# A one-core megakernel of retention, attention and channel mix: retention scores on 64-row halves, first row maxima on four banks, VectorE work reordered

## The chip, the cores and the metric

One core of one Trainium2 chip. The time is the device time of one execution in microseconds (us), and the metric is the median over runs. The engines are TensorE (PE in the profile, PEld for its weight loads), VectorE (DVE), ScalarE (ACT), GpSimd (POOL) and SyncE (SP), which issues most DMAs.

## The reference

Eight sequences of 1024 tokens with 256 channels, all in float32. What matters of it:

```
x = x + retention(layernorm(x))      # 4 heads, dk 64, dv 128
x = x + ffn(layernorm(x))            # channel mix: r * (relu(k)^2 @ W_v)
x = x + attention(layernorm(x))      # 16 heads of 16, relative bias, softmax
x = x + ffn(layernorm(x))

# retention, chunk by chunk (the kernel uses chunks of 128)
attn = (q @ k^T) * Dmask
o = attn @ v + (q * cross) @ S
S = S * gC + (k * kdec)^T @ v
o = rmsnorm(o) * silu(g);  out = x + o @ Wo
```

The attention's softmax subtracts the true maximum of each row of scores (query), so scores are computed twice: once by rows, to get the maxima, and once by columns (keys on partitions) with the maximum folded in as an extra row of the operands.

## The kernel before

Each sequence goes through five stages, and each engine's program is written out by hand, with semaphores (`need`, `reach`, `wait_ge`) between them. An engine runs its instructions in order, so the order written in the code is the order of the work. A product of plain float32 operands is two passes of PE, one with `F32R` operands is one.

**Retention** (loop `for t in range(1, NT + 1)` on PE; NT = 8 tiles of 128 tokens). DVE makes the normalised tile (`z_norms`, L1466), PE transposes it (`z_transposes`, L637), ACT copies it with the layer norm's weights (`z_copies`, L1310), and DVE takes the low part (`z_lows`, L1617). `project` (L643, L647) makes q and k (bank 0), v (bank 1) and the gate g (bank 2), six products of 512 columns each. DVE rotates q and k (`rope`, L1639 and L1645), POOL adds and scales (L1909, L1916), PE transposes them into bank 3 (`qk_transposes`, L1027), and ACT copies them out in three operations (L1358 to L1360): q of two heads goes to `qbd`, whose other halves are zeros, so that one product on all 128 rows serves two heads (block diagonal), and k goes to `kT`. For tile u = t - 1 PE then makes the scores (L1058, two products of 256 columns into bank 4), DVE masks them into `AT` (L1668), and PE makes the outputs in bank 5: per head `AT` times v (L1082) and, for u > 0, `qbd` times the state S (L1085). L1092 is the update of the state, on column halves (64 output rows each) of the array; DVE adds it to S (L1690, L1693). ACT squares the outputs (L1348), POOL makes the reciprocal root (L1924, L1928), ACT takes tanh of g (L1353), DVE makes the gate (L1703) and the gated outputs y (L1710). y is transposed (`y_transposes`, L977), copied and split (L1332, `y_lows` L1623), projected (`y_project`, L991, twelve products of 256 columns) and added to x (`x_out`, L1630), three tiles later.

**First channel mix** (`mix_k` L683, `mix_r` L707, `mix_kv` L725, with layer norms `ln_stats`, `ln_norms` L1590, `ln_transposes` L666, `ln_copies` L1257; POOL squares in L1863 and adds in L1872). **Attention's projections** (`qk_project` L831, `v_project` L843). SP spreads q and k to `SQ` and `SK` through DMAs, 64 rows of partitions for each head: even heads on partitions 0 to 63, odd ones on 64 to 127.

**Ahead stage** (`last_mix_and_rows`): the first AHEAD = 22 of 128 units of row products, put between the second channel mix of the sequence before. A unit is one head and one tile of queries, and has two products of 512 columns, k = 0 and 1 (`score_rows`, L868). DVE takes the maximum of each (`row_max`, L1755). Row products take banks 0 to 2 in turn. After 16 units the maxima of a block are folded (L1759), transposed (`max_transpose`, L882), copied (L1401) and written into `SQ` by DMA (`max_rows_in`, L450). In the DVE program statistics, norms, mixes and gated products of the sequence before are hung between the units by number.

**Attention** (64 steps): two more units of rows per step until all are done, four column products (`score_cols`, L899), exponentials on ACT (L1430), the bias band on POOL (L1964), and the weighting with v (`weigh`, L924), on column quarters. At its end the next sequence's first projections begin, with its `rope(b + 1, 0)`.

In the set-up of the first sequence DVE makes constants (L1516 to L1521) and the bias tables (`bias_tables`, L1548 to L1558) ahead of its loop.

## Time and profile before

| | us |
|---|---|
| median of 3 runs | 2854.99 (2853.36 to 2856.19) |
| the profiled execution, its own time | 2854.48 |
| its span in the profile | 2852.6 |
| PE busy | 2752.4 |
| DVE busy | 2115.9 |
| ACT busy | 1775.8 |
| POOL busy | 1266.7 |

Busy time of PE counts from a matmul's start to its modelled end; as matmuls are pipelined, the next one starts before that, and a row of the timeline with several of them (x8) shows the start of the first and the time to the end of the last. So the distance between the starts of two rows is what the first of them took. [...] The rows below are mostly from one inner sequence, the one whose retention stage begins at 1066.6 us.

### The profile page before, as it was taken

The numbers are of one execution on the slowest core, as the hardware profiler recorded it, in microseconds if no ns is written. First come the engines' busy times: TensorE is split into PE (matmuls) and PEld (weight loads), VectorE is DVE, ScalarE is ACT, GpSimd is POOL, SyncE is SP. The second block draws the span as 40 slices with busy tenths as digits, with TensorE's granted clock in tenths as the row PEclk, the third lists the DMA queues.
The fourth block names the chain that finished last, engine by engine and source line by source line (L and its number), as shares of the span: only waits on it lengthen the run. The fifth ranks groups of instructions, "written<-read, shape, count | busy, mean of one in ns | idle before, by whom it ended". The sixth has DMA issues, their size and how long they took to land.

```text
span 2852.6 us, 53205 instructions
## 1 busy us (share of the span) xinstructions
PE 2752.4 (96%) x19426; PEld 1526.9 (54%) x19426; DVE 2115.9 (74%) x4444; ACT 1775.8 (62%) x3799; POOL 1266.7 (44%) x1764
## 2 busy tenths in 40 slices
PE   7989999999999999999999999999999999999998
PEld 5733376433864348643486434854358533585334
DVE  6679756897568965689666995669956799567993
ACT  5438854488545875458754687536875378653785
POOL 3415544355433554335543445434454345433553
PEclk9979999999999999999999999999999999999999
DMA  7160001600025000250002400033000330003300
GB/s 191 31 133 2 24 9 41 137 17 24 9 50 128 17 31 1 60 119 17 31 1 74 105 17 31 1 90 88 17 31 10 101 69 17 31 30 89 60 2 16
DMA packets 71428, 139.16 MB, mean 49 GB/s; under 512 B 12784, under 2 KB 49696, under 8 KB 70016
## 3 DMA queue, kind: packets, MB, share of 16 engines
q1 hardware_dynamic: 69152, 135.29, 19.1%
q8 instruction: 156, 2.56, 0.4%
q14 instruction: 104, 0.85, 0.1%
q10 hardware_dynamic: 2016, 0.45, 0.1%
HBM read 86.02 MB, written 38.82 MB: 44 GB/s over the span
## 4 chain that ended last, share of the span: by engine, by line
PE 71%; DVE 14%; issue 6%; POOL 5%; SPq 1%; ACT 1%; DMA 1%; POOLq 0%; DVEq 0%; ACTq 0%
PE psum L868 20%; PE psum L924 16%; DVE mx L1755 6%; PE psum L643 5%; PE psum L991 3%; PE psum L899 3%; PE psum L831 3%; PE psum L647 2%; PE psum L707 2%; PE psum L683 2%; PE psum L1085 2%; PE psum L1082 2%; DVE nrm L1590 2%; PE psum L1058 1%; POOL X L1872 1%
## 5 line engine op out<-in xcount | busy, mean ns | idle before, releaser
L1755 DVE TENSOR_REDUCE mx<-psum 128x1 f32<-128x512 f32 x2048 | 1266.2, 685 | 87.4 <-PE psum L868 87.0
L1430 ACT ACTIVATE Z<-psum 128x512 f32<-128x512 f32 x2048 | 1109.6, 598 | 279.7 <-PE psum L899 252.6
L1964 POOL TENSOR_TENSOR Z<-Z,W_low 128x256 f32<-128x256 f32 (+1 forms) x1152 | 713.0, 642 | 687.2 <-ACT Z L1430 679.9
L868 PE MATMUL psum<-SK,SQ 63*128 63x512 f32 x2048 | 801.2, 471 | 28.5 <-DVE mx L1755 23.0
L899 PE MATMUL psum<-SQ,SK 64*128 64x512 f32 x2048 | 758.6, 472 | 8.1 <-DMA SQ<-mrow 7.5
L924 PE MATMUL psum<-Z,Vx 128*17 128x256 f32 x8192 | 642.0, 388 | 0.4 <-POOL Z L1964 0.4
L868 PEld LDWEIGHTS psum<-SK,SQ 63*128 63x128 f32 x2048 | 330.0, 191 | 480.8 <-DVE mx L1755 357.9
L899 PEld LDWEIGHTS psum<-SQ,SK 64*128 64x128 f32 x2048 | 311.4, 189 | 79.9 <-ACT Z L1430 37.5
L924 PEld LDWEIGHTS psum<-Z,Vx 128*17 128x17 f32 x8192 | 138.3, 95 | 334.8 <-issue 274.8
L1909 POOL TENSOR_TENSOR Z<-Z 128x512 f32<-128x512 f32 x64 | 83.6, 1306 | 295.6 <-DVE Z L1645 295.6
L1872 POOL TENSOR_TENSOR X<-X,mixed 128x512 f32<-128x512 f32 x64 | 80.4, 1268 | 235.3 <-DVE mixed L1611 235.3
L643 PE MATMUL psum<-W_high,zT_both 128*128 128x512 f32 x384 | 170.2, 443 | 0.5 <-ACT Z L1310 0.5
L643 PE MATMUL psum<-W_low,zT_both 128*128 128x512 f32 x384 | 152.2, 396 | 0.0
L1348 ACT ACTIVATE Z<-psum 128x128 f32<-128x128 f32 x256 | 67.2, 277 | 125.0 <-PE psum L1085 122.6
L683 PE MATMUL psum<-xkT,WT 128*128 128x512 f32 x256 | 126.3, 613 | 4.0 <-DVE xkT L1601 2.1
L707 PE MATMUL psum<-WT,xrT 128*128 128x256 f32 x512 | 126.5, 389 | 0.0
L831 PE MATMUL psum<-nT,WT 128*128 128x512 f32 x256 | 115.8, 600 | 6.6 <-ACT nT L1257 6.6
L647 PE MATMUL psum<-W_high,zT_both 128*128 128x512 f32 x384 | 120.1, 394 | 0.0
L1283 ACT ACTIVATE mixed<-psum 128x512 f32<-128x512 f32 x64 | 38.2, 597 | 130.0 <-PE psum L707 130.0
L707 PEld LDWEIGHTS psum<-WT,xrT 128*128 128x128 f32 x512 | 92.6, 189 | 32.4 <-issue 22.6
L1590 DVE TENSOR_SCALAR nrm<-X,fmv,frs 128x256 f32<-128x256 f32 x192 | 73.8, 446 | 43.7 <-POOL frs L1858 43.7
L1310 ACT ACTIVATE zT_both<-psum,vec 128x128 fp32r<-128x128 f32 x128 | 51.6, 454 | 83.8 <-PE psum L637 83.3
(138 smaller groups left out, 3716.8 us busy)
## 6 DMA issues: line engine op xcount, KB each, us to landing
W_low<-bias_rows SPq DMA_DIRECT2D x8, 2048.0 KB, 8.6
parts<-Z SPq DMA_DIRECT2D x32, 512.0 KB
W_low<-low_parts SPq DMA_DIRECT2D x7, 1536.0 KB, 6.7
X<-L_attn_a_x SPq DMA_DIRECT2D x8, 1024.0 KB, 5.6
SQ<-parts SPq DMA_DIRECT2D x32, 256.0 KB, 7.9
SK<-parts SPq DMA_DIRECT2D x32, 256.0 KB, 10.7
SQ<-parts SPq DMA_DIRECT2D x16, 512.0 KB, 6.6
SK<-parts SPq DMA_DIRECT2D x16, 512.0 KB, 14.5
```

What stands on the lines that cost most here:

```text
L643: pe.matmul(bank[dst], zT_parts[0][:, t % 2, c, :], Wqkvg_parts[part][:, c, c0:c0 + 512], start=c == 0 and part == 0, stop=False)
L647: mm = pe.matmul(bank[dst], zT_parts[1][:, t % 2, c, :], Wqkvg_parts[0][:, c, c0:c0 + 512], start=False, stop=c == C - 1)
L683: mm = pe.matmul(k_bank(b, q, o), WT[:, W_K, c, o * P:o * P + P], xkT[:, c, :], start=c == 0, stop=c == C - 1)
L707: mm = pe.matmul(bank[4 + pr][:, i * D:i * D + D], xrT[:, c, t * P:t * P + P], WT[:, W_R, c, :], start=c == 0, stop=c == C - 1)
L831: mm = pe.matmul(bank[QK_BANK[n % 2]], WT[:, A_Q + side, c, h * P:h * P + P], nT[:, c, 1 + 512 * g:513 + 512 * g], start=c == 0, stop=c == ...
L868: pe.matmul(row_bank(c), SQ[rows_of(h, MAX_ROW), h // 2, i * P:i * P + P], SK[rows_of(h, MAX_ROW), h // 2, 512 * k:512 * k + 512], start=T ...
L899: pe.matmul(col_bank(n), SK[rows_of(h), h // 2, j * P:j * P + P], SQ[rows_of(h), h // 2, 512 * half:512 * half + 512], start=True, stop=Tr ...
L924: mm = pe.matmul(sum_bank(s // 8)[32 * c:32 * c + HD + 1, cols], Vx[:, j, 4 * hg + c, :], ring[:, (4 * s + cols_of(s).index(c)) % RING, cols],
L1430: nc.scalar.activation(ring[:, n % RING, :], col_bank(n), ACT.Exp)\
L1590: nc.vector.tensor_scalar(nrm[:, i, :], X_of[b % 2][:, 4 * g + i, :], fmv[:, i, 0:1], frs[:, i:i + 1], ALU.subtract, ALU.mult).then_inc(fn ...
L1755: nc.vector.tensor_reduce(mx2[:, blk % 2, col, k:k + 1], row_bank(2 * u + k), AX_X, ALU.max)\
L1964: nc.gpsimd.tensor_tensor(ring[:, n % RING, a:z], ring[:, n % RING, a:z], band_exp[:, 4 * hg + cols_of(s)[i], at:at + z - a], ALU.mult)\
```

## The change

- `qbd` and `kT` give way to one tile `qkT` (q and k of the tile, all 128 rows, no zeros), which ACT fills with one copy. Two heads of a pair lie on its rows 0 to 63 and 64 to 127. The scores are now, in the new function `scores`, four products of 128 columns on 64 rows each, for the even heads into bank 4 and for the odd ones into bank 5. q times S follows in the same function, also on 64 rows, into the columns 256 to 511 of the same banks; `outputs` adds `AT` times v to it. DVE masks both banks in one operation (`by_side`), and ACT and DVE read the outputs with `o_of(h)`.
- PE's order in a tile: the v projection goes ahead of the scores; from tile 3 on the next transposes of z stand between them. At t = 2 the states go ahead of the outputs. `scores` waits for the gated outputs of the tile before.
- DVE's order: `rope(b, t)` ahead of the mask, `rope(b, 1)` out of the loop, behind the last norm of the sequence's start (in the first sequence ahead of `constants` and `bias_tables`); `ln_stats(b, 0)` and `ln_norms(b, 0)` earlier, the gated outputs at t = 7 ahead of the gate; `z_norms(b, 3)` at t = 1.
- Ahead stage: `row_product` orders the first 44 row products so that the same k of two units follows one another, and with that two halves of the rows; banks 0 to 3 in turn for the first 40 of them. The layer norm of the second half of the mix (`ln_transposes(b - 1, 5)`) stands earlier, on banks 6 and 7; mixes and gated products hang at other units; the first block's transpose goes to bank 4.
- In the last mix `mix_kv` waits for the copies of that norm, and ACT makes them ahead of the tanhs.

The diff, cut to its core:

```diff
-qbd = sb("qbd", [P, 2, 2, 2, P])
+qkT = sb("qkT", [P, 2, 4, P])
...
-LN_BANK = (0, 0, 0, 0, 4, 3)
+LN_BANK = (0, 0, 0, 0, 4, 6)
...
+def o_of(h):
+
+    return bank[4 + h % 2][:, 256 + h // 2 * DV:256 + h // 2 * DV + DV]
+
...
+def row_product(c):
+    if c < 2 * AHEAD:
+        return c // 4 * 2 + c % 2, c % 4 // 2
+    return c // 2, c % 2
+ROW_BANKS = [c % 4 if c < 2 * AHEAD - 4 else c % 3 for c in range(2 * NU)]
+LAST_ROW = [max((m for m in range(c) if ROW_BANKS[m] == ROW_BANKS[c]), default=None) for c in range(2 * NU)]
 def row_bank(c):
-    return bank[c % 3]
+    return bank[ROW_BANKS[c]]
...
-            need(pe, c_lo, min(b + 1, B - 1), 8)
+            pe.wait_ge(k_relu, 2 * mix_at(b, 2) + 2)
         for c in range(C):
-            if n == 5 and c == 1:
-                pe.wait_ge(r_tanh, 2 * mix_at(b, 2) + 1)
...
+        if q == 2:
+            pe.wait_ge(fn_T, 2 * norm_at(b, 5) + 2)
...
-            for u in range(rows, rows + n):
-                score_rows(b, u, 0)
-                score_rows(b, u, 1)
+            for c in range(2 * rows, 2 * rows + 2 * n):
+                score_rows(b, c)
...
             mix_r(b - 1, 2, 0, (0,))
             some_rows(1)
+            ln_transposes(b - 1, 5)
             mix_r(b - 1, 2, 0, (1,))
...
-            ln_transposes(b - 1, 5)
...
-        if b > 0:
+            mix_kv(b - 1, 3, 0, (0,))
+            max_transpose(b, 0)
+            some_rows(1)
+            mix_kv(b - 1, 3, 0, (1,))
+            some_rows(1)
             mix_kv(b - 1, 3, 1, (0,))
             some_rows(1)
             mix_kv(b - 1, 3, 1, (1,))
+        else:
+            some_rows(17 - rows)
+            max_transpose(b, 0)
         some_rows(AHEAD - rows)
...
+
+        u, k = row_product(c)
         h, i, _, _ = unit(u)
-        c = 2 * u + k
         if k == 0:
             rows_wait(b, u)
         if c == 0:
             pe.wait_ge(fn_T, 2 * norm_at(b, 3) + 2)
-        elif c > 2:
-            need(pe, mx_r, b, c - 2)
+        if c == 3:
+            need(pe, c_lo, b, 8)
+        if LAST_ROW[c] is not None:
+            need(pe, mx_r, b, LAST_ROW[c] + 1)
...
+        if n == 0:
+            need(pe, mx_r, b, 2 * AHEAD - 4)
...
+    def scores(b, u):
+        need(pe, kq_T, b, u + 1)
+        need(pe, att_m, b, u)
+        need(pe, s_upd, b, 2 * u)
+        need(pe, y_h, b, 4 * u)
+        if u == 0:
+            need(pe, z_T, b, 8)
+            need(pe, w_T, b - 1, 1)
+        for pr in range(2):
+            for side in range(2):
+                r = slice(DK * side, DK * side + DK)
+                mm = pe.matmul(bank[4 + side][:, P * pr:P * pr + P], qkT[r, u % 2, 2 + pr, :],
+                               qkT[r, u % 2, pr, :], start=pr == 0, stop=False, skip_group_check=True)
+        if u > 0:
+            for pr in range(2):
+                for side in range(2):
+                    r = slice(DK * side, DK * side + DK)
+                    mm = pe.matmul(o_of(2 * pr + side), qkT[r, u % 2, pr, :], S[r, pr, :],
+                                   start=False, stop=False, skip_group_check=True)
+        mm.then_inc(att.sem, 1)
+    def outputs(b, u):
+        need(pe, att_m, b, u + 1)
+        need(pe, v_cp, b, u + 1)
+        for h in range(RET_HEADS):
+            mm = pe.matmul(o_of(h), AT[:, h * P:h * P + P], v_sb[:, u % 2, h * DV:h * DV + DV],
+                           start=False, stop=h >= 2, skip_group_check=True)
+        mm.then_inc(p_o.sem, 1)
+    def states(b, u):
+        need(pe, v_cp, b, u + 1)
+        need(pe, s_upd, b, 2 * u)
+        need(pe, z_T, b, 4 * min(u + 3, NT))
+        for h in range(RET_HEADS):
+            mm = pe.matmul(bank[6][64 * (h % 2):64 * (h % 2) + 64, (h // 2) * DV:(h // 2) * DV + DV],
+                           qkr[:, u % 2, 256 + h * DK:256 + h * DK + DK],
+                           v_sb[:, u % 2, h * DV:h * DV + DV], start=True, stop=True,
+                           skip_group_check=True)
+        mm.then_inc(p_st.sem, 1)
...
+            u = t - 1
+            if t == 1:
+                scores(b, u)
+            if t <= 2:
                 z_transposes(b, t + 1)
+            if t < NT:
                 need(pe, v_cp, b, t)
                 if t == 1:
                     need(pe, x_att, b - 1, 3)
                 project(b, t, 1, 512, p_v)
+            if 3 <= t < NT - 1:
+                z_transposes(b, t + 1)
+            if t >= 2:
+                scores(b, u)
+            if t >= 3:
                 y_project(b, t - 3)
             if t == NT:
                 y_transposes(b, NT - 2)
+            if t == 2:
+                states(b, u)
+            outputs(b, u)
+            if t != 2 and t < NT:
+                states(b, u)
             if t < NT:
...
-                quad = bank[3].rearrange("p (a n) -> p a n", a=4)
-                nc.scalar.copy(qbd[0:64, t % 2, :, 0, :], quad[0:64, 0:2, :]).then_inc(kq_T.sem, 1)
-                nc.scalar.copy(qbd[64:128, t % 2, :, 1, :], quad[64:128, 0:2, :]).then_inc(kq_T.sem, 1)
-                nc.scalar.copy(kT[:, t % 2, :, :], quad[:, 2:4, :]).then_inc(kq_T.sem, 1)
+                nc.scalar.copy(qkT[:, t % 2, :, :], bank[3].rearrange("p (a n) -> p a n", a=4)).then_inc(kq_T.sem, 1)
...
+    def by_side(w):
+
+        return w[:, :].rearrange("p (c a n) -> p a c n", a=2, c=2)
...
     z_lows(0, 1)
     z_norms(0, 2)
+    rope(0, 1)
     constants()
     bias_tables()
     for b in range(B):
         for t in range(NT + 1):
-            if 1 < t < NT - 1:
+            if 2 < t < NT - 1:
                 z_norms(b, t + 1)
             if 3 <= t and t != 7:
                 y_lows(b, t - 3)
+            if 2 <= t < NT:
+                rope(b, t)
             if 1 <= t:
                 u = t - 1
                 need(dve, att, b, u + 1)
                 need(dve, p_o, b, u)
-                nc.vector.tensor_tensor(AT[:, :], bank[4], mask[:, :], ALU.mult)\
+                nc.vector.tensor_tensor(by_side(AT), psum[:, 4:6, 0:256].rearrange("p a (c n) -> p a c n", c=2),
+                                        by_side(mask), ALU.mult)\
                     .then_inc(att_m.sem, 1)
-            if 0 < t < NT:
-                rope(b, t)
+            if t == 1:
+                z_norms(b, 3)
             if t >= 3:
                 x_out(b, t - 3)
             if 0 < t < NT - 1:
                 z_lows(b, t + 1)
+            if t == 6:
+                ln_stats(b, 0)
+            if t == 7:
+                ln_norms(b, 0)
...
             if t == 7:
-                ln_norms(b, 0)
+                gated_outputs(b, u)
             if b == 0 and 3 <= t < 7:
                 bias_rows(2 * t - 5)
             if t < NT:
-                need(dve, p_g, b, t + 1)
-                need(dve, g_tanh, b, t + 1)
-                nc.vector.scalar_tensor_tensor(gt[:, t % 2, :], gt[:, t % 2, :], 1.0, bank[2],
-                                               ALU.add, ALU.mult).then_inc(gate.sem, 1)
-            if 1 <= t <= NT:
-                need(dve, o_rs, b, u + 1)
-                need(dve, gate, b, u + 1)
-                need(dve, y_tp, b, u)
-                for h in range(RET_HEADS):
-                    nc.vector.scalar_tensor_tensor(y[:, h * DV:h * DV + DV], bank[5][:, h * DV:h * DV + DV],
-                                                   ors[:, u % 2, h:h + 1], gt[:, u % 2, h * DV:h * DV + DV],
-                                                   ALU.mult, ALU.mult).then_inc(y_h.sem, 1)
+                gates(b, t)
+            if 1 <= t <= NT and t != 7:
+                gated_outputs(b, u)
...
-                    mixes(b - 1, 3, (0,), (0,))
-                elif u == 8:
-                    mixes(b - 1, 3, (0,), (1,))
+                    mixes(b - 1, 3, (0,))
+                elif u == 9:
                     gated(b - 1, 2, (0,))
-                elif u == 9:
+                elif u == 10:
                     gated(b - 1, 2, (1,))
-                elif u == 11:
+                elif u == 12:
                     mixes(b - 1, 3, (1,))
-                elif u == 16:
+                elif u == 18:
                     gated(b - 1, 3, (0,))
-                elif u == 17:
+                elif u == 20:
                     gated(b - 1, 3, (1,))
...
             z_lows(b + 1, 1)
             z_norms(b + 1, 2)
+            rope(b + 1, 1)
...
-                need(pool, att, b, t)
+                need(pool, p_st, b, max(t - 1, 0))
```

## Rows read from the trace of the kernel before

**Rows 1.** The page: span, and busy time of the engines.

```profile
span 2852.6 us, 53205 instructions
...
PE 2752.4 (96%) x19426; PEld 1526.9 (54%) x19426; DVE 2115.9 (74%) x4444; ACT 1775.8 (62%) x3799; POOL 1266.7 (44%) x1764
```

**Rows 2.** The page: the chain that ended last, by line.

```profile
PE psum L868 20%; PE psum L924 16%; DVE mx L1755 6%; PE psum L643 5%; PE psum L991 3%; PE psum L899 3%; PE psum L831 3%; PE psum L647 2%; PE psum L707 2%; PE psum L683 2%; PE psum L1085 2%; PE psum L1082 2%; DVE nrm L1590 2%; PE psum L1058 1%; POOL X L1872 1%
```

**Rows 3.** Busy time by stretch: us, engines' busy us (instructions), clock, DMA.

```profile
1066.60:1149.60 83.00, 81.94 (x535) 70.30 (x532) 49.48 (x129) 42.98 (x138) 33.53 (x40) 1.00 0.02 6
...
1201.60:1244.80 43.20, 41.98 (x142) 22.82 (x142) 36.08 (x67) 9.91 (x17) 10.96 (x10) 1.00 0.55 146
...
1209.80:1246.50 36.70, 35.41 (x124) 19.68 (x123) 29.68 (x50) 8.83 (x16) 9.02 (x8) 0.99 0.58 155
...
1246.50:1387.00 140.50, 138.37 (x1287) 50.97 (x1285) 136.08 (x252) 120.34 (x226) 74.91 (x120) 0.98 0.15 31
```

**Rows 4.** Waits in 1201.6 to 1244.8: who for whom, us, times, longest.

```profile
DVE mx L1755 <- PE psum L868: 5.9, 8, 2.0
```

**Rows 5.** Timeline, PE, tile 0 and 1 of retention: start us, us, instruction.

```profile
1080.13 1.05 PE L1082 MATMUL psum<-Z 128*128 128x128 f32 x8
...
1081.11 0.66 PE L1092 MATMUL psum<-Z 128*64 128x128 f32 x8
...
1082.04 0.39 PE L643 MATMUL psum<-W_low,zT_both 128*128 128x512 f32 x1
...
1084.09 0.66 PE L1027 MATMUL psum<-ident,Z 128*128 128x128 f32 x4 [0.74 <-POOL Z L1916]
```

**Rows 6.** Timeline, PE, a tile of retention with a state.

```profile
1115.08 1.03 PE L1058 MATMUL psum<-qbd,Z 128*128 128x256 f32 x4
...
1115.94 0.38 PE L637 MATMUL psum<-ident,Z 128*128 128x128 f32 x2
...
1118.96 0.38 PE L1082 MATMUL psum<-Z 128*128 128x128 f32 x2
...
1120.84 0.66 PE L1092 MATMUL psum<-Z 128*64 128x128 f32 x8
```

**Rows 7.** Timeline, ACT and DVE, the same stretch.

```profile
1110.84 0.28 ACT L1348 ACTIVATE Z<-psum 128x128 f32<-128x128 f32 x1 [2.60 <-PE psum L1085]
...
1114.32 1.12 DVE L1710 SCALAR_TENSOR_TENSOR Z<-psum,ors,Z 128x128 f32<-128x128 f32 x4
...
1116.28 0.68 DVE L1668 TENSOR_TENSOR Z<-psum,mask 128x512 f32<-128x512 f32 x1
```

**Rows 8.** Timeline, PE and DVE, ahead stage.

```profile
1209.93 1.13 PE L707 MATMUL psum<-WT,xrT 128*128 128x256 f32 x4
...
1210.99 0.73 PE L868 MATMUL psum<-SK,SQ 63*128 63x512 f32 x2
...
1211.65 1.13 PE L707 MATMUL psum<-WT,xrT 128*128 128x256 f32 x4
...
1241.01 5.47 DVE L1755 TENSOR_REDUCE mx<-psum 128x1 f32<-128x512 f32 x9
```

**Rows 9.** Timeline, PE, attention stage, two products on opposite halves.

```profile
702.73 0.49 PE L899 MATMUL psum<-SQ,SK 64*128 64x512 f32 x2
```

**Rows 10.** Timeline, PE and DVE, set-up of the first sequence.

```profile
30.07 0.62 PE L647 MATMUL psum<-W_high,zT_both 128*128 128x512 f32 x2
...
27.80 0.29 DVE L1516 TENSOR_SCALAR nrm<-nrm,vec 128x128 f32<-128x128 f32 x1 [0.54 <-DMA cbias<-L_attn_b_bo]
...
32.26 0.41 DVE L1558 COPY xrT<-xrT 64x64 f32<-64x64 f32 x2
...
35.01 1.05 PE L1082 MATMUL psum<-Z 128*128 128x128 f32 x8
```

**Rows 11.** Busy time by stretch, as in 3: first sequence, and one attention begin.

```profile
157.10:193.70 36.60, 26.77 (x56) 12.56 (x56) 27.46 (x46) 0.96 (x3) 0.00 (x0) 0.59 0.54 150
...
1246.00:1252.90 6.90, 6.90 (x28) 2.96 (x28) 6.10 (x11) 5.31 (x11) 4.20 (x6) 0.51 1.05 156
```

More of the change, by code:

```diff
@@ L424, in max_bank @@
         def max_bank(blk):
-            return sum_bank(blk) if blk else bank[3]
+            return sum_bank(blk) if blk else bank[4]
         def rows_of(h, n=HALF):
@@ L692, in mix_r @@
                 reach(pe, r_tanh, 2 * at + pr - 1)
-                if q == 0 and pr == 0:
-                    need(pe, att_m, b, NT)
-                if q == 0 and pr == 1:
+                if q == 0:
                     need(pe, y_h, b, 4 * NT)
@@ L875, in max_transpose @@
                 if blk == 0:
-                    need(pe, c_lo, b, 8)
-                    pe.wait_ge(fn_T, 2 * (norm_at(b - 1, 5) if b > 0 else norm_at(b, 3)) + 2)
+                    need(pe, vx_cp, b, 4)
+                    if b > 0:
+                        pe.wait_ge(r_tanh, 2 * mix_at(b - 1, 3) + 1)
                 elif blk == 1:
@@ L1106, in _ @@
                 need(pe, gate, b, NT)
-                need(pe, kq_T, b, 3 * NT)
+                need(pe, kq_T, b, NT)
                 mix_k(b, 0, 0)
@@ L1347, in _ @@
                         for h in range(RET_HEADS):
-                            nc.scalar.activation(sq_junk[:, h * DV:h * DV + DV], bank[5][:, h * DV:h * DV + DV], ACT.Square,
+                            nc.scalar.activation(sq_junk[:, h * DV:h * DV + DV], o_of(h), ACT.Square,
                                                  accum_out=oss[:, u % 2, h:h + 1]).then_inc(o_sq.sem, 1)
@@ L1487, in ln1_scales @@
                     .then_inc(ln1_sc.sem, 1)
-            for dst, value in ((power[:, :], -0.5), (nT[:, :, 0:1], 0.0), (qbd[:, :, :, :, :], 0.0),
+            for dst, value in ((power[:, :], -0.5), (nT[:, :, 0:1], 0.0),
                                (Vx[:, :, :, HD:HD + 1], 1.0), (S[:, :, :], 0.0), (nrm[:, 0, :], 1.0)):
@@ L1646, in rope, with gates, gated_outputs @@
                         .then_inc(rope_ab.sem, 1)
+            def gates(b, t):
+                need(dve, p_g, b, t + 1)
+                need(dve, g_tanh, b, t + 1)
+                nc.vector.scalar_tensor_tensor(gt[:, t % 2, :], gt[:, t % 2, :], 1.0, bank[2],
+                                               ALU.add, ALU.mult).then_inc(gate.sem, 1)
+            def gated_outputs(b, u):
+                need(dve, o_rs, b, u + 1)
+                need(dve, gate, b, u + 1)
+                need(dve, y_tp, b, u)
+                for h in range(RET_HEADS):
+                    nc.vector.scalar_tensor_tensor(y[:, h * DV:h * DV + DV], o_of(h),
+                                                   ors[:, u % 2, h:h + 1], gt[:, u % 2, h * DV:h * DV + DV],
+                                                   ALU.mult, ALU.mult).then_inc(y_h.sem, 1)
             z_lows(0, 0)
@@ L1749, in _, with row_max @@
                         mixes(b - 1, 2, (1,))
-                def row_max(u):
-                    _, _, blk, col = unit(u)
-                    for k in range(2):
-                        need(dve, mx_s, b, 2 * u + k + 1)
-                        nc.vector.tensor_reduce(mx2[:, blk % 2, col, k:k + 1], row_bank(2 * u + k), AX_X, ALU.max)\
+                def row_max(n):
+                    for c in (2 * n, 2 * n + 1):
+                        u, k = row_product(c)
+                        _, _, blk, col = unit(u)
+                        need(dve, mx_s, b, c + 1)
+                        nc.vector.tensor_reduce(mx2[:, blk % 2, col, k:k + 1], row_bank(c), AX_X, ALU.max)\
                             .then_inc(mx_r.sem, 1)
-                    if u % 16 == 15:
-                        need(dve, mx_r, b, 2 * u + 2)
+                    if n % 16 == 15:
+                        need(dve, mx_r, b, 2 * n + 2)
                         nc.vector.tensor_reduce(mx[:, blk, :], mx2[:, blk % 2], AX_X, ALU.max).then_inc(mx_f.sem, 1)
```

66 lines of the change are left out of this document (11 added, 55 removed).

## The prediction

> **What bounds the kernel now.** I read the page first, then the chain, the stage table, the waits, and last the timeline. TensorE (PE) is busy 96% of 2852.6 us [rows 1], but its ends are modelled, so the chain decides: it runs through PE matmuls, and the row-maximum line of VectorE (DVE) is its third place [rows 2]. The stages of one inner sequence [rows 3] then differ. In the retention stage (83.0 us) PE is busy 81.94 and its weight loads 70.30; DVE only 49.48. In the ahead stage (43.2 us, 22 units of first row products between the previous sequence's channel mix) DVE has 36.08. In the attention stage DVE has 136.08 of 140.5: the row maxima bound it, and whatever ends the ahead stage's maxima earlier should move all that follows. In the ahead stage DVE waits 5.9 us for row products [rows 4]: PE is the later one there.
>
> **Retention, PE work removed.** A full-array pass of 128 columns follows the next in 0.111 us: eight take 0.98 us to the first of the state update, which includes the step into column halves [rows 5]. Scores before are two products of 256 columns, 0.86 us [rows 6]. The outputs of a tile with a state are 16 passes in 1.88 us, 0.1 of it the same step, so 1.78 [rows 6]; eight of them are q times S on a half-empty array. After, scores and q times S are 16 passes on 64 rows, even heads in bank 4 and odd in bank 5. If two run side by side that is 8 x 0.111 = 0.89 us in place of 0.86 + 0.89 = 1.75. No row shows 64-row passes of this kind, but two neighbours do the same thing: the state update, on column halves, takes its eight passes and the first projection product in 0.93 us where serial ones would need 8 x 0.111 + 0.23 = 1.12 before any overhead [rows 5], and two 512-column products on opposite row halves end within 0.49 us, two on one half within 0.73 [rows 8, 9].
>
> The step into and out of halves costs time. From the same rows: 0.98 - 0.89 = 0.09 going in, and 0.93 - 0.445 - 0.23 = 0.25 inside and coming out: 0.34 per visit. The new `scores` adds one visit per tile. So a tile with a state saves 1.75 - 0.89 - 0.34 = 0.52 us, the first tile 0.86 - 0.445 - 0.34 = 0.07. Per sequence 7 x 0.52 + 0.07 = 3.7 us. Bounds: nothing pairs (below), or the visit costs as little as 0.1 (2 us more per sequence).
>
> [...]
>
> **Retention, waits moved.** Scores of tile u now stand behind the v projection and overwrite what the outputs of u-1 were read from, so they wait for the gated outputs of u-1. That chain is squares on ScalarE (ACT), a power on GpSimd (POOL), four DVE products: 1110.84 to 1115.44, 4.6 us after the outputs end [rows 7]. PE has the states, gate projection, transposes, q/k and v projections, about 6 us, in between: hidden, with some 1.3 us over. The mask (0.68 [rows 7], about 1.0 with the latency of PE's last pass) lies behind the y projection (12 x 0.115 = 1.4 us) from the fourth tile on: hidden. At t = 2 only the state update (0.6) covers it: 0.3 lost. At t = 8 DVE does gated outputs, gate and the low part of y in a row (1.12 + 0.69 + 0.68, forms as in [rows 7]) before PE can go on with the y projection: 0.7 lost. One copy in place of three after the q/k transposes frees ACT, which isn't late anyway: nothing. The second rope moved ahead of the loop takes away the 0.74 us (0.9 with the restart) that PE waits for POOL at t = 1 [rows 5], in seven sequences. Net per inner sequence 3.7 - 0.3 - 0.7 + 0.9 = 3.6; seven make 25 us. No DMA is moved or added.
>
> **The first sequence's set-up.** rope(0, 1) now stands ahead of the constants and bias tables on DVE and waits for a projection that ends at 30.7. The constants and tables took 27.80 to 32.67, in DVE's idle time [rows 10]; now rope takes 1.45 and they follow: 30.75 + 1.45 + 4.9 = 37.1. Gate and mask (0.69 + 0.68) end at 38.6, and the outputs that ran at 35.01 [rows 10] start at 38.7: 3.7 later. The rest of that sequence's gain (3.7 - 1.0 + 0.4) pays most of it; with PE idle some 4 us I add 1.5 for a possible fall of the clock. Net 2 us lost. [...]
>
> **The ahead stage.** Between 1209.93 and 1211.65 PE does four passes (0.86 us) and one unit of rows: the unit costs 0.86 us, of which 0.46 are two products one after the other (k = 0 and 1 of one head, one half) and 0.40 switching [rows 8]. In the new order `some_rows(1)` issues the same k of an even and an odd head, which pair: 0.23 + about 0.30 = 0.53. 22 units save 7.3 us of PE. Added up from 1202.2: before 23.3 us of other matmuls + 22 x 0.86 = 42.2, which is the stage's length; after 35. DVE's own work there, 44 maxima at 0.608 (nine in 5.47 us [rows 8]) = 26.8, statistics 1.8, norms 1.4, mixes 2.8, gated products 2.7, takes 35.5 from 1203.2: it would end at 1238.7 without a wait, and ends at 1246.5 now. So DVE becomes the bound. Going through the new order unit by unit (four banks let PE be two units ahead; transposes of norm 5 on banks 6 and 7, ready right after unit 5; r mixes late by 1.8 us at unit 14, PE waiting), I get the last maximum at 1241.1: 5.4 us earlier. I take 5.0; bounds 2 and 7.7 (all of DVE's idle time, 36.7 - 29.7 [rows 3], and a little at its start). Seven sequences: 35 us. In the first sequence DVE and the copy-in of the row maxima bound the stage: nothing. The attention stage itself is unchanged and moves ahead whole. The last sequence's mix loses 1.5 us: its second half now waits for two ACT copies of norm 5 before the product with W_V (two operations near the 0.7 of [rows 7]).
>
> **Sum.** -25 + 2 - 35 + 1.5 = -56.5 us. The profiled execution took 2854.5 (span 2852.6), 0.5 below the median of the runs, 2855.0. 2854.5 - 56.5 = **2798 us**.
>
> **Rivals.**
> (A) The 64-row passes don't pair. Then each tile with a state gives 0.89 back, the first 0.445: 6.7 a sequence, 53 in all: 2851, within 0.2% of before. For it: no row has 128-column passes with a 128-column load each on row halves, and two loads must fit in 0.11 us. Against: [rows 5, 9]. Chance 0.04.
> (B) The ahead stage gives little, because DVE or the load of the row maxima holds the attention stage's begin (2 us instead of 5 a sequence, less where mixes are late): 21 less, 2819; with further waits in retention, up to 2832. For it: the margin between PE's 35.0 and DVE's 35.5 is nothing, so every late mix shows. Chance 0.15.
> (C) Slower: the clock. [...] Chance 0.05.
> **Numbers.** Main case 0.76 (its own range 2784 to 2814, from the bounds of visit and ahead stage), B 0.15, A 0.04, C 0.05. 0.2% (5.7 us) is what a measurement can tell from no change. Faster 0.92, same 0.03, slower 0.05. The range leaves out the low tail, A and C, and takes in B: 2782 to 2832.
>
> **What would show it.** Right: in a steady tile the new line of the scores has 16 passes in about 1.2 us; the tile's period falls from 10.1 to 9.6; `L1027` has no wait at t = 1; a unit of rows in the ahead stage costs 0.5 us and DVE has hardly any wait there; retention 79.5 and ahead stage 38 us long; DVE ends its first 44 maxima 5 us earlier; PE idle 4 us around 35 to 38. Wrong: passes at 0.111 each in the scores (A); PE waiting for gated outputs or mask in every tile; granted clock below 1 inside the ahead stage (C); ACT or a load ending the wait of the first column product (B).

## The result and the profile after

The changed kernel takes **2825.38 us** (median of 4 runs, 2824.51 to 2830.58) against 2855.26 for the kernel before on the same chip: ratio 0.9901, 95% interval 0.9889 to 0.9913. Of the 57 us forecast, 30 came. The direction was right, the time lies in the range, and the size was wrong: about half.

The page of after, span and engines, then the chain by line:

```profile
span 2822.7 us, 53686 instructions
...
PE 2696.9 (96%) x19682; PEld 1476.0 (52%) x19682; DVE 2143.4 (76%) x4443; ACT 1741.6 (62%) x3671; POOL 1252.9 (44%) x1764
...
PE psum L882 18%; PE psum L941 16%; DVE mx L1809 8%; PE psum L655 7%; PE psum L1008 3%; PE psum L659 3%; PE psum L916 3%; PE psum L715 2%; PE psum L1064 2%; PE psum L977 2%; PE psum L842 2%; DVE nrm L1628 2%; POOL X L1926 1%; PE psum L1049 1%; DVE xrT L1639 1%
```

In the kernel after, L1049 is the scores, L1055 q times S, L1064 the outputs, L882 the row products, L1809 their maxima, L916 the column products, L941 the weighting with v, L715 the r products and L1639 the mixes of DVE. PE is busy some 55 us less than in [rows 1], and the span is 30 shorter. A new line stands at the end of the chain, `xrT L1639`, a mix of DVE.

The stages were measured in both traces from the first instruction of one to that of the next (q/k/v projection, q/k products of attention, first row product, first column product):

| us, before and after | before | after | change | forecast |
|---|---|---|---|---|
| retention and first mix, sequence 0 | 116.5 | 119.2 | +2.7 | +2 |
| the same, seven others together | 793.5 | 762.7 | -30.8 | -25 |
| ahead stage, seven others together | 303.4 | 296.4 | -7.0 | -35 |
| ahead stage of sequence 0, and all q/k products | 207.9 | 208.8 | +0.9 | 0 |
| attention stages of sequences 0 to 6 | 1203.5 | 1206.0 | +2.5 | 0 |
| end of the last sequence | 208.6 | 210.2 | +1.6 | +1.5 |

So the retention stage gave more than forecast, and the ahead stage almost nothing. The windows of after show it: an ahead stage (1191.2), its slow part, another ahead stage (1536.9), and the attention stage behind that (columns as in [rows 3]; the third number from the end is the granted clock, a share of full speed, as a mean over the window):

```profile
1191.20:1235.00 43.80, 40.68 (x143) 22.12 (x142) 36.99 (x66) 9.83 (x17) 9.29 (x9) 0.92 0.51 137
1218.80:1225.60 6.80, 6.75 (x16) 4.27 (x16) 2.48 (x4) 0.60 (x1) 0.00 (x0) 0.50 0.52 213
1536.90:1577.60 40.70, 37.52 (x143) 20.36 (x142) 37.05 (x66) 9.83 (x17) 9.40 (x9) 1.00 0.56 149
1577.60:1718.00 140.40, 137.61 (x1262) 50.61 (x1262) 135.47 (x249) 119.41 (x223) 74.91 (x119) 0.98 0.17 35
```

The first is longer than the 43.20 of [rows 3] although PE has less work; the second, of the same instructions, is 3.1 us shorter. What parts them is 6.8 us at a granted clock of 0.50. Five of the seven ahead stages of after have such a stretch (three of 3.4 us, two of 6.8); [rows 3] has a clock of 1.00 over the whole stage. The timeline of PE ahead of it:

```profile
1203.80 0.49 PE L882 MATMUL psum<-SK,SQ 63*128 63x512 f32 x2
1204.23 1.13 PE L715 MATMUL psum<-WT,xrT 128*128 128x256 f32 x4
1205.29 0.49 PE L882 MATMUL psum<-SK,SQ 63*128 63x512 f32 x2
...
1216.35 0.49 PE L882 MATMUL psum<-SK,SQ 63*128 63x512 f32 x2
1218.85 2.08 PE L715 MATMUL psum<-WT,xrT 128*128 128x256 f32 x4 [2.00 <-DVE xrT L1639]
1220.86 0.80 PE L882 MATMUL psum<-SK,SQ 63*128 63x512 f32 x2
1221.58 3.78 PE L715 MATMUL psum<-WT,xrT 128*128 128x256 f32 x8
```

PE waits 2.00 us for a mix of DVE (an "r mix", which makes the input `xrT` of the r products). After it the same four r products take 2.01 us (to 1220.86) instead of the 1.06 at 1204.23. DVE at that time:

```profile
1198.27 2.10 DVE L1628 TENSOR_SCALAR nrm<-X,fmv,frs 128x256 f32<-128x256 f32 x4
...
1215.40 1.29 DVE L1809 TENSOR_REDUCE mx<-psum 128x1 f32<-128x512 f32 x2 [1.00 <-PE psum L882]
1216.61 2.19 DVE L1639 SCALAR_TENSOR_TENSOR xrT<-nT,vec,xrT 128x512 f32<-128x512 f32 x2
1218.72 1.27 DVE L1809 TENSOR_REDUCE mx<-psum 128x1 f32<-128x512 f32 x2
1221.68 1.29 DVE L1809 TENSOR_REDUCE mx<-psum 128x1 f32<-128x512 f32 x2 [1.69 <-PE psum L882]
1225.97 0.69 DVE L1809 TENSOR_REDUCE mx<-psum 128x1 f32<-128x512 f32 x1 [3.00 <-PE psum L882]
```

The mixes begin only at 1216.61, behind unit 12, and take 2.19 us, where the same two take 1.41 in the kernel before (at 1226.46 there); then DVE, which should have become the bound, waits 1.69 and 3.00 us for row products that PE makes late. All seven stages have the wait of 1.99 or 2.00 us, the two without a fall too:

```profile
1564.56 1.13 PE L715 MATMUL psum<-WT,xrT 128*128 128x256 f32 x4 [2.00 <-DVE xrT L1639]
1565.62 0.50 PE L882 MATMUL psum<-SK,SQ 63*128 63x512 f32 x2
```

The steady tile of retention, timeline of PE, to be read against [rows 6]:

```profile
1098.86 0.72 PE L1049 MATMUL psum<-qkT 64*128 64x128 f32 x8
1099.40 0.61 PE L1055 MATMUL psum<-S,qkT 64*128 64x128 f32 x8
1099.95 0.74 PE L1008 MATMUL psum<-W_high,yT_both 128*128 128x256 f32 x4
1100.53 0.63 PE L1008 MATMUL psum<-W_low,yT_both 128*128 128x256 f32 x4
...
1101.47 1.05 PE L1064 MATMUL psum<-Z 128*128 128x128 f32 x8
...
1108.48 0.72 PE L1049 MATMUL psum<-qkT 64*128 64x128 f32 x8
```

16 passes in 1.09 us (1098.86 to 1099.95), and a tile every 9.62 us.

### The profile page after: what moved, and what is told of

It is laid out like the page before. It is cut to its first block, busy times and chain, and to the rows that moved or that the text cites. A ratio compares the mean times of both kernels' runs of the same rounds, so it can differ in the third digit from the quotient of the medians.

```text
span 2822.7 us, 53686 instructions
## 1 busy us (share of the span) xinstructions
PE 2696.9 (96%) x19682; PEld 1476.0 (52%) x19682; DVE 2143.4 (76%) x4443; ACT 1741.6 (62%) x3671; POOL 1252.9 (44%) x1764
## 4 chain that ended last, share of the span: by engine, by line
PE 70%; DVE 17%; POOL 4%; issue 4%; ACT 2%; SPq 1%; DMA 1%; POOLq 0%; DVEq 0%; ACTq 0%
PE psum L882 18%; PE psum L941 16%; DVE mx L1809 8%; PE psum L655 7%; PE psum L1008 3%; PE psum L659 3%; PE psum L916 3%; PE psum L715 2%; PE psum L1064 2%; PE psum L977 2%; PE psum L842 2%; DVE nrm L1628 2%; POOL X L1926 1%; PE psum L1049 1%; DVE xrT L1639 1%
## 5 line engine op out<-in xcount | busy, mean ns | idle before, releaser
L1809 DVE TENSOR_REDUCE mx<-psum 128x1 f32<-128x512 f32 x2048 | 1265.5, 684 | 81.9 <-PE psum L882 81.1
L882 PE MATMUL psum<-SK,SQ 63*128 63x512 f32 x2048 | 761.2, 474 | 31.0 <-DVE mx L1809 26.1
L916 PE MATMUL psum<-SQ,SK 64*128 64x512 f32 x2048 | 756.3, 469 | 9.3 <-DMA SQ<-mrow 8.8
L941 PE MATMUL psum<-Z,Vx 128*17 128x256 f32 x8192 | 642.0, 388 | 0.4 <-POOL Z L2018 0.4
L882 PEld LDWEIGHTS psum<-SK,SQ 63*128 63x128 f32 x2048 | 309.0, 190 | 481.3 <-DVE mx L1809 368.0
L916 PEld LDWEIGHTS psum<-SQ,SK 64*128 64x128 f32 x2048 | 309.0, 188 | 81.4 <-ACT Z L1464 37.4
L941 PEld LDWEIGHTS psum<-Z,Vx 128*17 128x17 f32 x8192 | 138.3, 95 | 334.1 <-issue 275.6
L715 PE MATMUL psum<-WT,xrT 128*128 128x256 f32 x512 | 135.2, 409 | 14.0 <-DVE xrT L1639 14.0
L715 PEld LDWEIGHTS psum<-WT,xrT 128*128 128x128 f32 x512 | 98.3, 201 | 42.1 <-DVE xrT L1639 16.2
L1628 DVE TENSOR_SCALAR nrm<-X,fmv,frs 128x256 f32<-128x256 f32 x192 | 77.9, 467 | 43.7 <-POOL frs L1912 43.7
```

The costliest lines, as they stand in the source:

```text
L715: mm = pe.matmul(bank[4 + pr][:, i * D:i * D + D], xrT[:, c, t * P:t * P + P], WT[:, W_R, c, :], start=c == 0, stop=c == C - 1)
L882: pe.matmul(row_bank(c), SQ[rows_of(h, MAX_ROW), h // 2, i * P:i * P + P], SK[rows_of(h, MAX_ROW), h // 2, 512 * k:512 * k + 512], start=T ...
L916: pe.matmul(col_bank(n), SK[rows_of(h), h // 2, j * P:j * P + P], SQ[rows_of(h), h // 2, 512 * half:512 * half + 512], start=True, stop=Tr ...
L941: mm = pe.matmul(sum_bank(s // 8)[32 * c:32 * c + HD + 1, cols], Vx[:, j, 4 * hg + c, :], ring[:, (4 * s + cols_of(s).index(c)) % RING, cols],
L1628: nc.vector.tensor_scalar(nrm[:, i, :], X_of[b % 2][:, 4 * g + i, :], fmv[:, i, 0:1], frs[:, i:i + 1], ALU.subtract, ALU.mult).then_inc(fn ...
L1809: nc.vector.tensor_reduce(mx2[:, blk % 2, col, k:k + 1], row_bank(c), AX_X, ALU.max)\
```

## The experiments

The theory after the result: the retention gain is real pairing; in the ahead stage the mixes behind unit 12 reach PE 2 us late, and the wait also brings the clock down. Rivals: the ahead stage's reorder is worth little by itself because DVE is full; the clock falls because PE has less to do, wherever the mixes are; the retention gain comes from something else than the halves. The kernel before was run beside every set of kernels, and its medians lie between 2854.06 and 2855.94 us: differences between kernels of different sets are good to about 2 us.

### The two halves of the change

`ret_only` is the changed kernel with the ahead stage, its banks, its DVE order and the last mix as before; `ahead_only` is the kernel before with these alone changed.

```diff
-LN_BANK = (0, 0, 0, 0, 4, 6)
+LN_BANK = (0, 0, 0, 0, 4, 3)
...
-    return bank[ROW_BANKS[c]]
+    return bank[c % 3]
```

> The changed kernel with its ahead stage as before (row products of one head in a row, three banks, norm 5 and mixes where they were); retention, set-up and rope stay changed. My theory now: the retention part gives all I had put on it and a little more, 4.4 us in each of seven inner sequences, less 4 us in the first: about 2828 us, and the ahead stage gives the little that is left. Rival (the parts need each other: the ahead stage's gain pays for a retention loss): clearly above 2835 us. The granted clock should not fall before the last 5 us of an ahead stage.

Measured: 2827.66 (2825.46 to 2829.90), ratio 0.9904 [0.9890, 0.9917]. As the theory has it: within the noise the retention side and the set-up are the whole of the measured gain.

> The kernel before with only the ahead stage changed (paired row products, four banks, norm 5 earlier, mixes at other units). My theory: it gives 0 to 1.5 us a sequence and costs 1.5 at the end of the last, 2845 to 2855 us. If the ahead stage were worth the 5 us a sequence that I forecast and retention took it back, it would be near 2822 us. [...]

Measured: 2851.29 (2843.80 to 2861.84, 11 runs), ratio 0.9993 [0.9981, 1.0006]: no difference that can be measured. All seven ahead stages of the profiled run have the same wait of 2.0 us; five are 40.5 to 40.7 us long, and the first (42.1) and the last (43.7) have a fall of the clock to 0.50 behind it, of 3.4 and 6.8 us. The runs spread over 18 us, and the mean granted clock goes with them: 0.984 in the fastest (2843.80), 0.978 in the slowest (2861.84).

### The place of the r mixes

`mix_11` moves one item of DVE's order by one unit. Behind unit 12 the r mixes stand after two row maxima that wait 1.00 us for PE (1215.40 above). Theory 1 was that PE's wait of 2.0 us for these mixes brings the clock down: behind unit 11 the wait is gone and the granted clock 1.00 up to the end of every ahead stage, 2 to 4 us a sequence, 2800 to 2812 us.

```diff
-elif u == 12:
+elif u == 11:
     mixes(b - 1, 3, (1,))
```

> The changed kernel with the r mixes of the second half one unit earlier on VectorE (behind unit 11, not 12). [...] Theory 2 (VectorE bounds the stage anyway, the wait only shows its backlog): the wait moves to the next row products, and the time stays within 4 us of 2825.

Measured: 2804.70 (2803.55 to 2806.57), ratio 0.9824 [0.9810, 0.9837]: 20.7 us less than after. The timeline of PE in `mix_11`, at the place of the wait:

```profile
1207.93 0.51 PE L882 MATMUL psum<-SK,SQ 63*128 63x512 f32 x2
1208.37 1.13 PE L715 MATMUL psum<-WT,xrT 128*128 128x256 f32 x4
1209.43 0.50 PE L882 MATMUL psum<-SK,SQ 63*128 63x512 f32 x2
1209.86 1.99 PE L715 MATMUL psum<-WT,xrT 128*128 128x256 f32 x8
```

No wait and no fall (granted clock 1.00 in all seven ahead stages), though the mixes still take 2.2 us and DVE is as busy as in after (36.96 us here, 37.05 in the window from 1536.9 above):

```profile
1205.90 2.21 DVE L1639 SCALAR_TENSOR_TENSOR xrT<-nT,vec,xrT 128x512 f32<-128x512 f32 x2
...
1524.60:1563.30 38.70, 37.52 (x144) 20.42 (x143) 36.96 (x66) 9.84 (x17) 9.50 (x9) 1.00 0.53 143
```

The ahead stages are 38.6 to 39.0 us. The theory holds; the rival that DVE is full falls, and so does the one that less work brings the clock down by itself.

`fill` is the changed kernel with the late mixes where they are, and lets PE make four throwaway products (128x256, plain float32) in the 2.0 us that it waits for them; nothing of the computation is left out:

```diff
+pe.wait_ge(r_tanh, 2 * mix_at(b - 1, 3) - 1)
+for i in range(4):
+    pe.matmul(bank[4][:, 0:D], ident[:, :], WT[:, W_R, 0, :], start=True, stop=True)
 mix_r(b - 1, 3, 0, (0,))
```

> [...] Theory (the clock falls because of that wait): granted clock 1.0 until the last 5 us of every ahead stage, and 1.5 to 3 us gained in the sequences in which it fell, about 2812 to 2820 us. Rival (the fall comes from the paired row products, wherever TensorE waits): the clock falls in the middle of the stage as before, and the time is 2825 or a few us more.

Measured: 2815.37 (2813.12 to 2815.96), ratio 0.9859 [0.9846, 0.9873]. The mixes come as late as before, but PE is at work until then (the four products from 1211.66, the r products at 1213.73), and the granted clock is 1.00 in all seven ahead stages, which are 40.5 to 41.0 us long. So the falls of the clock cost 10.0 of the 20.7 us, and the wait itself the other 10.7 (`fill` and `mix_11` are of one set; the kernel before took 1.2 us less beside them than beside after, and the 10.0 may hold that much of the chips' difference).

`best_fill` is the control: the same filler in the best kernel (`m11_setup`, below), where there is no wait to fill.

> The m11_setup kernel with the four throwaway 128x256 products of the fill run ahead of the r product of the fourth quarter, where PE now has no wait. If fill gained through the clock alone, it has nothing left to gain here, and the products cost what they take, at most 0.9 us a sequence where PE sets the end: 2796 to 2802. If filler helps for another reason, the time falls below 2793.

Measured: 2805.00 (2803.48 to 2805.38), ratio 0.9824 [0.9809, 0.9838]: some 8 us slower. The same filler gained 10.0 us where it stood in a wait of 2.0 us. My price for it was a miss: the four float32 products are eight passes (x8 in the row) and take 1.83 us (1206.45 to 1208.28), not 0.9.

```profile
1206.45 1.99 PE L797 MATMUL psum<-WT,ident 128*128 128x256 f32 x8
1208.28 1.03 PE L715 MATMUL psum<-WT,xrT 128*128 128x256 f32 x4
```

`m8_setup` and `m10_setup` have the r mixes behind unit 8 and unit 10, ahead of one or both gated products of the third quarter, in the kernel `m11_setup`:

```diff
-elif u == 11:
+elif u == 8:
     mixes(b - 1, 3, (1,))
```

> As m11_setup, with the r mixes behind unit 8, next to the k mixes, when GpSimd has nothing to do. Theory (the r mixes take 2.2 us in place of 1.4 because GpSimd squares at the same time): they take 1.4 us, 0.8 us a sequence, 2792 to 2796 us. Rival (other work of VectorE, earlier by three units, keeps TensorE from row banks or gated products, so the gain is eaten): 2798 to 2806 us.

Measured: 2806.55 (2802.38 to 2807.43), ratio 0.9829 [0.9815, 0.9842], 10.5 us slower than `m11_setup`. The mixes take 1.40 us there (from 1195.94; POOL is idle from 1186.6 to 1199.2), and PE waits for the gated product instead, 1.67 us in each of the seven stages. In one of them, of 41.6 us where the others have 39.9 to 40.2, the granted clock falls to 0.50 behind it for 3.4 us: four products take 3.34 us (2230.47 to 2233.81) instead of 1.92.

```profile
1199.19 1.12 PE L693 MATMUL psum<-xkT,WT 128*128 128x512 f32 x2 [1.67 <-DVE mixed L1649]
1200.67 1.98 PE L693 MATMUL psum<-xkT,WT 128*128 128x512 f32 x4
...
2228.78 1.12 PE L693 MATMUL psum<-xkT,WT 128*128 128x512 f32 x2 [1.67 <-DVE mixed L1649]
2230.47 3.41 PE L693 MATMUL psum<-xkT,WT 128*128 128x512 f32 x4
```

> The m11_setup kernel with the r mixes behind unit 10 and the second gated product of the third quarter behind unit 11. Behind unit 8 they were 10 us dearer because both gated products came late for PE; here only the second comes late, by 1.4 to 2.2 us, and PE needs it one product after the first. If PE waits for it by 0.5 to 1 us a sequence, 2799 to 2803; if the r mixes behind unit 11 are still late by a little and this is hidden, 2793 to 2796.

Measured: 2815.16 (2813.35 to 2820.89), ratio 0.9866 [0.9851, 0.9881], 18 us slower than the same kernel with 11. I expected 3 to 7; PE now waits for the gated product that was put behind the mixes, and the same two prices come back, here in the timeline of PE:

```profile
1204.19 1.12 PE L693 MATMUL psum<-xkT,WT 128*128 128x512 f32 x2
1207.05 1.13 PE L693 MATMUL psum<-xkT,WT 128*128 128x512 f32 x2 [1.74 <-DVE mixed L1649]
1208.10 0.50 PE L882 MATMUL psum<-SK,SQ 63*128 63x512 f32 x2
1208.54 1.75 PE L693 MATMUL psum<-xkT,WT 128*128 128x512 f32 x2
```

1.74 us of wait, then a product that takes 1.67 (to 1210.21) in place of 1.05: the granted clock fell to 0.50 at 1208.9 for 3.4 us, and in two more of the seven stages for 3.4 and 6.8 us. In this kernel the mixes themselves take 1.44 us (from 1203.76; POOL is idle from 1204.0 on), and it doesn't help. So it isn't the mix as such: both the r mixes and the gated product, when they reach PE 1.7 to 2.0 us late in this stage, cost their wait, and in part of the cases the clock. Behind unit 11 is the only one of the four places tried where PE has neither wait.

### The set-up

`m11_setup` is `mix_11` with the first rope behind the constants and tables again; `setup_back` is the changed kernel with that alone:

```diff
-rope(0, 1)
 constants()
 bias_tables()
+rope(0, 1)
```

> The changed kernel with the r mixes behind unit 11 and, in the first sequence, the second rope behind the constants and bias tables again. TensorE waited 5.7 us there for the mask, and the clock fell for 6.8 us after it. Theory (that wait is the whole cost of the set-up order): 4 us from the wait and 1 to 3 from the clock, 2797 to 2800 us. Rival (the time comes back later, since the first sequence's ahead stage waits for DMAs): 2804 us, as the r mixes alone gave.

Measured: 2796.08 (2795.53 to 2800.34), ratio 0.9798 [0.9785, 0.9811]. Repeated beside later kernels (`m11_again`):

> The same kernel as m11_setup, to be compared with the two others on one chip: 2796, within 3 us.

Measured: 2797.24 (2795.41 to 2802.69), ratio 0.9800 [0.9787, 0.9813].

> The changed kernel with the first sequence's rope(0, 1) behind the constants and tables again, and nothing else: the r mixes stay behind unit 12. If the set-up's cost is a thing of its own, it gives the same 8.6 us as beside mix_11: 2816.8. If part of the 8.6 came through the earlier r mixes, less: up to 2821. The forecast on record priced the late outputs at 2.2 us (3.7 less 1.5 for the clock counted apart: 5.2 with it): by that price 2820 to 2822.

Measured: 2816.64 (2814.14 to 2821.32), ratio 0.9863 [0.9846, 0.9879]: 8.7 us less than after, as beside `mix_11` (8.6). The order of the set-up costs 8.7 us where the forecast had 5.2. The timeline of after shows both parts of the difference, DVE's constants and tables, then the outputs of PE:

```profile
32.11 1.52 DVE L1554 TENSOR_SCALAR nrm<-nrm,vec 128x128 f32<-128x128 f32 x2
...
32.27 1.28 POOL L1963 TENSOR_TENSOR Z<-Z 128x512 f32<-128x512 f32 x1 [5.57 <-DVE Z L1683]
...
34.16 0.97 DVE L1558 TENSOR_SCALAR vec<-vec 128x2 f32<-128x2 f32 x1
...
40.10 2.07 PE L1064 MATMUL psum<-Z 128*128 128x128 f32 x8 [5.65 <-DVE Z L1726]
```

and the window that begins ahead of them:

```profile
37.80:44.60 6.80, 4.50 (x20) 3.67 (x20) 3.25 (x10) 1.14 (x8) 1.00 (x2) 0.50 0.39 119
```

The rope released POOL's work, and beside it the small operations of DVE got longer: L1558 takes 0.97 us here and 0.17 in `m11_setup`, where it comes at 28.23 and POOL is idle from 26.8 on. PE starts the outputs at 40.10 instead of 35.01 [rows 10], 1.4 us later than forecast, and at a granted clock of 0.50 (eight passes in 2.07 us, 1.05 there).

### Does the array pair?

All of these are edits of `m11_setup`. `unpaired` takes the old order of the 44 row products on four banks; `banks3` keeps the new order and takes three banks.

```diff
-    if c < 2 * AHEAD:
-        return c // 4 * 2 + c % 2, c % 4 // 2
     return c // 2, c % 2
```

> As m11_setup, with the first 44 row products in the old order (k = 0 and 1 of one head, one half of the rows), still on four banks. Theory (pairing takes 0.24 us from each unit on TensorE and that is what the stage gained): 22 x 0.24 = 5 us more in each of seven sequences where TensorE bounds, 2825 to 2835 us. Rival (VectorE bounds the stage, the pairs are hidden): within 3 us of m11_setup.

Measured: 2820.43 (2819.26 to 2820.80), ratio 0.9879 [0.9866, 0.9893]. Pairing is worth 24.3 us; the ahead stage is 42.6.

> As m11_setup, with the row products of the ahead stage on three banks again, still paired. Theory (the fourth bank lets TensorE run ahead of VectorE while this does mixes and norms): 1 to 3 us a sequence lost, 2805 to 2820 us. Rival (pairs alone do it): within 3 us of m11_setup.

Measured: 2806.55 (2805.82 to 2809.04), ratio 0.9832 [0.9818, 0.9845]. The fourth bank is worth 10.5 us; the ahead stage is 40.5 to 40.9. So each half of the ahead change pays, once no wait covers it.

For the retention stage, `serial` issues the products of one side together, and `one_side` computes those of the odd heads from the rows of the even heads, so that all lie on one half of the array:

```diff
-    for pr in range(2):
-        for side in range(2):
+    for side in range(2):
+        for pr in range(2):
```

```diff
-            r = slice(DK * side, DK * side + DK)
+            r = slice(0, DK)
```

> The m11_setup kernel, with the scores and the q times S products of one side of the array issued together (even, even, odd, odd in place of even, odd, even, odd). The work is the same; only neighbours on opposite halves become rarer. If the halves pair (the reading of 16 passes in 1.09 us), each tile's 16 passes should take 1.4 to 1.7 us instead of 1.09, unless PE lets more than one product overtake: 0.3 to 0.6 us a tile, 17 to 34 us over 56 tiles, so 2813 to 2830 (m11_setup: 2796). If the gain of the retention stage comes from the shorter streams alone and not from pairing, nothing changes: 2796.

Measured: 2803.00 (2801.68 to 2805.70), ratio 0.9819 [0.9804, 0.9834]. A miss: 16 passes in 1.19 us, 0.10 more than 1.09; 56 tiles times 0.10 are 5.6 us of the 6 to 7 that it is slower.

```profile
1087.19 0.72 PE L1049 MATMUL psum<-qkT 64*128 64x128 f32 x8
1087.73 0.71 PE L1055 MATMUL psum<-S,qkT 64*128 64x128 f32 x8
1088.38 0.74 PE L1008 MATMUL psum<-W_high,yT_both 128*128 128x256 f32 x4
```

That left open whether there is any pairing in it, or only shorter passes.

> The m11_setup kernel, with the scores and q times S of the odd heads computed from the even heads' rows, so that all 16 passes of a tile lie on rows 0 to 63 of the array: odd heads' retention outputs are left out, the even ones stand in their place. Number and size of the instructions are the same. If the gain comes from two halves at work side by side, nothing pairs now: 16 passes in 1.78 us (16 x 0.111) in place of 1.09, 0.69 a tile, 56 tiles, 39 us: 2835. If a pass on 64 rows is simply shorter than one on 128, whatever its neighbour is (what the 1.19 us of the order even, even, odd, odd suggests), 1.1 to 1.3 us, 0 to 12 us: 2796 to 2808.

Measured: 2849.52 (2846.11 to 2854.18), ratio 0.9982 [0.9973, 0.9991]: 52 us slower than `m11_again`. 16 passes take 1.98 us (1094.28 to 1096.26):

```profile
1094.28 1.16 PE L1049 MATMUL psum<-qkT 64*128 64x128 f32 x8
1095.27 1.05 PE L1055 MATMUL psum<-S,qkT 64*128 64x128 f32 x8
1096.26 0.74 PE L1008 MATMUL psum<-W_high,yT_both 128*128 128x256 f32 x4
```

The halves do pair: 1.98 against 1.09, a factor of 1.8, and 56 tiles times 0.89 are 50 us. Rival A is excluded. `serial` says that the issue order need not alternate product by product for it.

### The end of the last sequence

`last_act` gives the last sequence the banks and the order of before for the fifth norm:

```diff
-                if q == 2:
+                if q == 2 and b < B - 1:
                     pe.wait_ge(fn_T, 2 * norm_at(b, 5) + 2)
```

> The m11_setup kernel, and in the last sequence alone the fifth norm's transposes on banks 3 and 4, its copies behind the tanhs on ScalarE, and no wait for them ahead of the product with W_V, as in the kernel before. The end of the last sequence, which became 1.6 us longer with the change, should get them back: 2794.5. If the length there comes from something else (the banks' other users), no change: 2796.

Measured: 2797.60 (2795.23 to 2802.98), ratio 0.9802 [0.9787, 0.9816]. Inconclusive: in the profile the last sequence is 379.0 us instead of 380.0, but the median doesn't show it. In `ret_only`, which also has the old order there, the end behind the first column product is 208.9 us, near the 208.6 of before.

## Why the prediction was half right

**Retention, work removed: right.** Forecast 1.23 us for scores and q times S with the visit to the halves, and 0.52 saved a tile. From the first score to the next row it is 1.09; the first four products of the y projection then take 0.58 us (1099.95 to 1100.53) instead of 0.47, so that it is 1.20 with the way out. The tile's period fell from 10.10 us (1115.08 [rows 6] to the next tile's scores) to 9.62: 0.48 saved.

**Retention, waits moved: right in sum.** The wait of 0.74 us at t = 1 [rows 5] is gone. At t = 2 PE waits 0.21 us for the mask (0.3 forecast). At t = 8 the scores wait 0.54 us for the gated outputs and the y projection 0.51 for its low part; as the y transposes wait 0.24 in place of 1.00, PE's waits there grew by 0.4 in all (0.7 forecast). Seven stages gave 30.8 us against 25: 4.4 each, where 3.6 were forecast.

**Set-up: right in kind, small in size.** The outputs are late by 5.1 us, not 3.7, since the operations of DVE beside POOL got longer (L1558 0.97 us instead of 0.17). The 1.5 us for the clock were a guess that no run shows; what the trace of after has is a clock of 0.50 for 6.8 us (37.80 to 44.60), with PE busy for 4.50 of them. By `setup_back` the order costs 8.7 us, not 5.2; as the rest of the sequence gained, the table has +2.7.

**The ahead stage: the step that failed.** It is the term of 7 x 5.0 = 35 us. The prediction saw the late r mixes ("late by 1.8 us at unit 14, PE waiting") and yet had the last maximum come 5.4 us earlier, as if the wait were nearly hidden and cost nothing beyond itself. What the runs put in its place, for one sequence, read from the first q/k product to the end of the 44th row maximum (65.7 us before):
- without a fall of the clock 63.7: 2.0 gained, not 5.4;
- with one, 65.2 (three sequences) and 66.8 (two). Seven sequences give 2 x 2.0 + 3 x 0.5 - 2 x 1.1 = 3.3 us, not 35;
- in `mix_11` 61.6: 4.1 gained, near the forecast of 5. So the mixes' place alone costs 2.1 us a sequence, and a fall of the clock 1.5 or 3.1 more;
- the 1.3 us between 4.1 and 5.4 are left for two terms of the sum that were too small, in `mix_11` as in after. A unit of rows costs PE 0.62 us, not 0.53 (1203.80 to 1205.29 is 1.49, less 0.86 for the r products [rows 8]): 2.0 us for 22 units. DVE's own work is some 37 us, not 35.5, since the norms take 2.10 and the r mixes 2.19 us in place of 1.38 and 1.41: 1.5 us. Both can't lie on the path in full; how the 1.3 us divide is not shown.

Of the 20.7 us between after and `mix_11`, 10.7 are the wait and 10.0 the falls that follow from it (by `fill`). Seven times 2.1 would be 14.7 for the wait: in the profiles the attention stages of `mix_11` take 1213.2 us and those of `fill` 1206.8, one of `mix_11` with a fall of the clock of its own. The rest of that difference stays open.

The forecast looked at the length of PE's wait alone, and not at the clock behind it, 0.50 for 3.4 or 6.8 us in five of the seven stages of after. Rival C had the clock, at 0.05, but as a thing of little work in the whole stage, not of a single gap. No run shows that: in `mix_11`, with the same paired products and no such wait, the granted clock is 1.00 in all seven. Rival B had the right sentence ("every late mix shows") and the right time, 2819 to 2832, but that time in part by luck: its upper half needed more waits in retention, where the stage gained more than forecast, and its 2 us a sequence in the ahead stage were 0.5. At 0.15 it was held too low, for the prediction itself wrote that the margin between PE and DVE "is nothing".

**Attention unchanged: right.** Its inner stages keep DVE as the bound (135.47 of 140.40 against 136.08 of 140.50 in [rows 3]). **End of the last sequence: the size fits**, +1.6. That the later copies make it is not shown: `last_act` has 210.1 us there and the other kernels with the changed order 209.5 to 211.7.

With the mixes behind unit 11 and the old set-up order the kernel takes 2796 us, 2.0% less than before and 1.0% less than the change as made. That it is the 2798 of the forecast is partly luck: retention gave some 6 us more and the ahead stage less.

## What to carry to other kernels

When work is taken from one engine in a stage where two are nearly even, go through the other engine's order item by item: one item a unit late can eat the whole gain, and a unit too early makes another late. A wait of TensorE of 2 us a sequence cost here 10.7 us by itself and 10.0 by the clock: look for such a wait in the profile, and price both. Work put ahead of other work on VectorE can also release GpSimd earlier. In the set-up here the operations of VectorE that then ran beside it got longer, L1558 from 0.17 to 0.97 us: price those too.

## What was unexpected of the hardware

- **A fall of the clock behind one gap.** A wait of 2.0 us in a stage where PE was otherwise at work had a stretch at 0.50 behind it in five of seven sequences in after, in six of seven in `setup_back` and in two of seven in `ahead_only`; a wait of 1.74 us (`m10_setup`) in three of seven, one of 1.67 us (`m8_setup`) in one. The stretch began between 0.5 us before the end of the wait and 1.9 us after it, and lasted 3.4 or 6.8 us. In the ten profiles whose ahead stages have no wait of PE over 0.61 us, `fill` and `mix_11` among them, it came in none of 70 stages. What decides between the cases with a wait is open.
- **VectorE beside GpSimd.** The r mixes take 2.19 us while POOL squares (1.11 us from 1217.13) and 1.40 to 1.44 when it is idle. The norms take 2.10 us (1198.27) with two squares of POOL beside them (1.04 us from 1197.48, 1.08 from 1199.14) and 1.38 in the kernel before (1208.51), where a square covers 0.3 us of them. Row maxima, which read PSUM, take 1.28 us for two beside POOL's add (1.26 us from 1211.49) and 1.29 with POOL idle (1204.33). What parts the maxima from the mixes and norms is not shown. In the kernel before, POOL started only late in the r mixes, and POOL's square took 1.54 us instead of 1.04:

```profile
1226.46 1.41 DVE L1601 SCALAR_TENSOR_TENSOR xrT<-nT,vec,xrT 128x512 f32<-128x512 f32 x2
...
1227.22 1.54 POOL L1863 TENSOR_TENSOR Z<-Z 128x512 f32<-128x512 f32 x1 [1.84 <-ACT Z L1272]
```

- **Opposite halves need not alternate.** For 16 passes on 64 rows the order even, even, odd, odd takes 1.19 us (`serial`), even, odd, even, odd 1.09 (after), and all on one half 1.98 (`one_side`). Four passes in a row on one half cost 0.10 us in 16 passes.
